# A post-norm block with routed experts: six batches instead of five in the first feed-forward pass

## The chip, the cores and the metric

The kernel runs on one core of one Trainium2 chip. The metric is device time in microseconds (us) of one execution. An execution that is profiled carries its own time, which need not be that of the runs without a profile.

## What is computed

The input is 8 batches of 256 tokens with 128 channels, float32. The reference, cut to its skeleton:

```python
x = layernorm(x + attn_A(x))            # 16 heads of 8, one key/value head, rotary, causal
h = x + attn_B(rmsnorm(x, g1))          # 16 heads of 64, 4 key/value heads, rotary, causal
y = h + moe(rmsnorm(h, g2))
out = layernorm(x + y)

def moe(x):                             # n = 2048 tokens
    logits = x @ router_w + router_b
    vals, idx = top_k(logits, 2);  scores = softmax(vals)
    oh  = one_hot(idx, 8)
    pos = cumsum(cumsum(oh, axis=0), axis=1)      # place of the token in its expert's queue
    emask = oh * (pos < 256)                      # an expert takes 255 at most
    m = max over the two choices of (emask * expert number)
    y = ff_m(x)                                   # one expert a token: gelu(x@w2 * x@w1) @ w3
    slot = where(token was taken, y, x)
    return sum of slot * scores
```

The place of a token in an expert's queue depends on all tokens before it, and on none after it. So the first batches can be routed before the last ones are known.

## The kernel before, in words

**Steps.** `step(s)` for s = -4 to 7 runs software-pipelined stages: both attentions of several batches interleave. In step s the second attention's scores and values are those of batch s (stage SB), and its output projection, residual, norm and router logits are those of batch s-1 (stage TB). Steps 6 and 7 are thin: the first attention has ended, and step 7 has only SB and TB. Step 7 also projects batch 7 itself (`project_out(7)` finishes batch 6, `project_out(NB)` batch 7). Every engine has its own instruction list in a fixed order, and waits on semaphores.

**The feed-forward** works on tiles of 128 slots, each slot a token, each tile one expert. It has two passes, `PASSES`: before, tiles 0 to 9 of the 16 token tiles (batches 0 to 4) and tiles 10 to 15 (batches 5 to 7). A pass of n token tiles needs n + 7 slot tiles at most, so `COUNT` is 17 and 13: 30 tiles, taken two at a time in 16 groups (`GROUPS`), 9 in the first pass, whose last has one tile, and 7 in the second.

**Routing of a pass** on VectorE (DVE): `first_choices` (L1463 to L1474, 13 instructions), then `counts` on TensorE (PE; L831, L834), `admit` (DVE, L1483 to L1492), `ranks` (PE, L845, L848), `slots` (DVE, L1516 to L1540; after L1528 the indices `sidx` are there), `shares` (DVE, L1499 to L1506). GpSimd (POOL) then writes the tokens to their slots in memory, one indirect DMA a token tile (`scatter`, L563, each waiting for the landing of the one before the last), loads the slots back four tiles at a time (`load_slots`, L571), and multiplies the tokens by the share that they keep (`keep_inputs`, L577). `turn_slots` (PE, L1071) and `take_slots` (ScalarE, ACT) transpose a group's slots, `find_experts` (L1081) loads its experts' numbers into registers, `up` (L1095) begins it. Then follow ACT's `copy`, DVE's `gate` (L1562), ACT's `gelu`, PE's `turn_hidden` (L1105), DVE's `take_hidden` (L1569), PE's `down` (L1115), DVE's `take_outputs` (L1577), and a DMA to memory (SyncE, SP).

**Where the first pass is routed.** `ROUTED[0]` is step 6: counts and ranks stand between the score and value matmuls of step 6, scatter and loads at the end of POOL's step 6.

**The end.** When all outputs of the first pass are in memory, POOL gathers them, one indirect DMA a token tile (`gather`, L583). DVE adds them in two parts (`add_outputs(0)` and `(1)`, L1598 and L1602) behind its work of groups 14 and 15, before it takes the last group's hidden values. The rows of the second pass are gathered after the last group; then come `add_outputs(2)`, `(3)`, the last layernorm (L1608 to L1615) and the output's DMA.

The lines that set this:

```python
NB0 = NB - 3
GATHERS = [(0, 5), (5, 10), (10, 13), (13, 16)]
FINAL = [(0, 10), (10, 13), (13, 16)]
ROUTED = [NB - 2, NB]
```

Of the kernel before, what the change touches and what calls it, by code (L numbers as in the profile page):

```python
# [32 lines left out]
NB, T, C = 8, 256, 128  # L33
# [8 lines left out]
CAP = NB * T // E  # L42
EPS_LN, EPS_RMS = 1e-5, 1e-6
NEG = -1e30
NB0 = NB - 3
PASSES = [(0, NB0 * NT), (NB0 * NT, NTILES)]
PARTS = PASSES
COUNT = [hi - lo + E - 1 for lo, hi in PASSES]
# [3 lines left out]
GROUPS = [(i, list(range(START[i] + k, START[i] + min(k + 2, COUNT[i])))) for i in range(2) for k in range(0, COUNT[i], 2)]  # L52
NG = len(GROUPS)
NG0 = (COUNT[0] + 1) // 2
CHUNKS_X = [[(START[i] + k, START[i] + min(k + 4, COUNT[i])) for k in range(0, COUNT[i], 4)] for i in range(2)]
GATHERS = [(0, 5), (5, 10), (10, 13), (13, 16)]
FINAL = [(0, 10), (10, 13), (13, 16)]
QA = DA * (H + 1)
QB = (H + HKV) * DB

# [19 lines left out]
AHEAD = {"PA": 4, "MA": 3, "SA": 3, "TA": 2, "PB": 2, "MB": 1, "SB": 0, "TB": -1}  # L80
FIRST = -AHEAD["PA"]
ROUTED = [NB - 2, NB]
IN_STEP = {NB - 2: {"bv0": [(NB - 2, "bv0"), (NB - 2, "cnt0")], "sm0": [(NB - 2, "sm0"), (NB - 2, "rk0")]},
           NB - 1: {"sm0": [(NB - 1, "ws00"), (NB - 1, "ws01")], "bv3": [], "bo0": [], "bo1": [], "xfT": [], "lg": [],
                    "sm1": [(NB, "xg0"), (NB - 1, "ws10"), (NB - 1, "ws11"), (NB - 1, "bv3"),
                            (NB - 1, "bo0"), (NB - 1, "bo1"), (NB, "bo0"), (NB, "bo1")]}}
BETWEEN = {(0, 0): [(NB - 1, "xfT")], (0, 1): [(NB - 1, "lg")], (1, 0): [(NB, "xfT")], (1, 1): [(NB, "lg")],
           (2, 1): [(NB, "cnt1")], (3, 1): [(NB, "rk1")]}

# [98 lines left out]
def build(nc, x, Wq, bq, Wk, bk, Wv, bv, Wo, bo, g1, g2, wq, wk, wv, wo, router_w, router_b,  # L188
          w1, w2, w3, cf, cb, out):
    with ExitStack() as ctx:  # L190
# [454 lines left out]
        def _(pe):  # L645
# [323 lines left out]
            def step(s):  # L969

                on = stages(s)
                if s == FIRST:
                    pe.wait_ge(x0_in, 16)
                if s == FIRST + 1:
                    pe.wait_ge(x_in, 16)
                    pe.wait_ge(c_in, C_IN)
                    pe.wait_ge(wo_in, 16)
                    pe.wait_ge(bias_in, BIAS_OPS)
                if s + AHEAD["MB"] == 0:
                    pe.wait_ge(prep, 3)  # L980
                if s + AHEAD["PB"] == 0:
                    pe.wait_ge(wb_in, WB_IN)
                if "SB" in on:
                    pe.wait_ge(n_dma, 32 * (s + 1))
                scores(s, 0)
                if "TA" in on:
                    turn_values(s)
                maxima_a(s, 0, 2)
                maxima(s, 0, 2)
                if "TA" in on:  # L990
                    turn_out(s)
                if "SB" in on:
                    pe.wait_ge(v_in, s + 1)
                values(s, 0)
                if s == ROUTED[0]:
                    counts(0)
                maxima_a(s, 2, 4)
                if "TA" in on:
                    project_out_a(s)
                maxima(s, 2, 4)  # L1000
                values(s, 1)
                weights(s, 0)
                if s == ROUTED[0]:
                    ranks(0)
                scores(s, 1)
                maxima_a(s, 4, 6)
                maxima(s, 4, 6)
                values(s, 2)
                maxima_a(s, 6, 8)
                max_rows_a(s, 0)  # L1010
                scores(s, 2)
                if "PB" in on:
                    pe.wait_ge(xn_in, s + AHEAD["PB"] + 1)
                    turn_x(s, "bx", xn)
                if "TB" in on and s < NB - 1:
                    project_out(s)
                maxima_a(s, 8, 10)
                maxima(s, 6, 8)
                if "PB" in on:
                    project(s, 0)  # L1020
                if "SA" in on:
                    scores_a(s, 0)
                maxima_a(s, 10, 12)
                if s == NB - 1:
                    turn_slots(0, *GROUPS[0])
                    find_experts(0)
                    weights(s, 1)
                    values(s, 3)
                    project_out(s)
                    project_out(NB)  # L1030
                else:
                    values(s, 3)
                    max_rows_a(s, 1)
                    weights(s, 1)
                maxima(s, 8, 12)
                if "PB" in on:
                    project(s, 1)
                if "SA" in on:
                    scores_a(s, 1)
                if "MB" in on:  # L1040
                    max_rows(s)
                if "PA" in on:
                    n = s + AHEAD["PA"]
                    turn_x(s, "ax", x_all[:, NT * n:NT * (n + 1), :])
                if "SA" in on:
                    values_a(s, 0)
                if "PA" in on:
                    project_a(s)
                if "TB" in on and s < NB - 1:
                    turn_tokens(s)  # L1050
                if "PB" in on:
                    turn_qk(s, 0)
                if "SA" in on:
                    scores_a(s, 2)
                if "TB" in on and s < NB - 1:
                    logits(s)
                if "PB" in on:
                    turn_qk(s, 1)
                if "SA" in on:
                    values_a(s, 1)  # L1060
                if "PA" in on:
                    turn_qk_a(s)
# [89 lines left out]
        def _(dve):  # L1152
# [466 lines left out]
            def between(n, half):  # L1619

                if (n, half) == (0, 1):
                    take_logits(NB - 1, NB - 2)
                if (n, half) == (1, 1):
                    take_logits(NB, NB - 1)
                    first_choices(1)
                if (n, half) == (2, 1):
                    admit(1)
                if (n, half) == (3, 1):
                    slots(1)
                if (n, half) == (8, 1):  # L1630
                    shares(*PASSES[1], 2)
                if (n, half) == (10, 1):
                    dve.wait_ge(z_in, NB)
                    add_kept(0, 5, 1)
                if (n, half) == (11, 1):
                    add_kept(5, 10, 1)
                if (n, half) == (12, 1):
                    add_kept(10, 16, 3)
                if (n, half) == (14, 1):
                    add_outputs(0)  # L1640
                if (n, half) == (15, 1):
                    add_outputs(1)
# [29 lines left out]
        def _(act):  # L1672
# [112 lines left out]
            def step(s):  # L1785
# [26 lines left out]
                exp(s, 5)  # L1812
                if "TB" in on and s < NB - 1:
                    inverse_root(root_t, var_t, ln_t, r0_t, m + 1)
                if s == NB - 1:
                    take_slots(0, GROUPS[0][1])
                if "SA" in on:
                    exp_a(s, 0)
                    exp_a(s, 1)
# [58 lines left out]
                nc.scalar.activation(hid[:, n % 2, 0:t, :], gated[:, n % 2, 0:t, :], ACT.Gelu).then_inc(hid_in, 1)  # L1878

            nc.scalar.preload_act_table_set("gelu_and_others")  # L1880
            for n, (i, g) in enumerate(GROUPS):
                copy(n, g)
                if n < 2:
# [30 lines left out]
```

## Time and profile before

| | |
|---|---|
| median of 3 runs | 573.47 us (573.19 to 574.51) |
| the profiled execution's own time | 579.19 us |
| its span | 577.3 us |
| PE busy | 481.7 us, 83% |
| DVE, ACT, POOL busy | 387.3 us (67%), 227.8 us (39%), 161.6 us (28%) |
| step 7's first score matmul, from the span's start | 454.61 us |
| first `up` of the feed-forward | 485.43 us |
| last `down` ends | 555.9 us |

The span is the time from the first to the last record; the execution's own time has 1.9 us around it. All times of day below count from the span's start.

### The profile page before, as it was taken

What the parts mean: (1) busy time and instruction counts of PE and PEld (TensorE: products, weight loads), DVE (VectorE), ACT (ScalarE), POOL (GpSimd) and SP (SyncE); (2) the same over time, 40 slices, a digit from 0 to 9 for tenths busy, and PEclk for the clock granted to TensorE, in tenths of its full rate; (3) what the DMA queues carried; (4) which work ended last, traced back from release to release, by engine and by line L of the source; (5) the groups of instructions that cost most, each with busy time, mean ns of one, the idle gap of its engine ahead of it and who ended that gap; (6) DMA issues with size and microseconds to landing.
All of it is one profiled execution on the core that took longest, in us unless ns stands there. A gap on an engine that the chain in (4) does not pass through costs nothing.

```text
span 577.3 us, 8112 instructions
## 1 busy us (share of the span) xinstructions
PE 481.7 (83%) x2788; PEld 266.8 (46%) x2788; DVE 387.3 (67%) x1096; ACT 227.8 (39%) x420; POOL 161.6 (28%) x200
## 2 busy tenths in 40 slices
PE   3766887799999999999999999999879688978820
PEld 2324353454354545535553645455445336645520
DVE  3517779757768676686767686676876266755585
ACT  1242351554473354427424733642333232435300
POOL 4210411400413241124304232222335360062521
PEclk9978997999999999999999999999889799999965
DMA  7400000000020003000300200030341520031213
GB/s 212 157 2 1 1 2 1 3 1 1 3 64 14 0 4 76 1 3 3 73 2 3 63 13 2 3 74 1 119 104 33 154 86 1 19 112 36 74 43 89
DMA packets 19093, 23.82 MB, mean 41 GB/s; under 512 B 2630, under 2 KB 15374, under 8 KB 18158
## 3 DMA queue, kind: packets, MB, share of 16 engines
q1 hardware_dynamic: 15308, 18.19, 12.0%
q0 software_dynamic: 1648, 4.07, 2.5%
q10 hardware_dynamic: 2098, 1.05, 0.6%
q8 instruction: 23, 0.38, 0.3%
q14 instruction: 16, 0.13, 0.1%
HBM read 16.71 MB, written 6.28 MB: 40 GB/s over the span
## 4 chain that ended last, share of the span: by engine, by line
PE 64%; DVE 14%; ACT 9%; issue 5%; DMA 4%; POOL 2%; ACTq 1%; another core or an unknown queue 0%; POOLq 0%; DVEq 0%; SPq 0%
PE ps_r L929 8%; PE ps_st L894 6%; PE ps_r L956 6%; PE ps_r L661 5%; PE ps_r L803 4%; ACT pt L1689 4%; PE ps_st L883 4%; PE ps_r L784 3%; PE ps_r L945 3%; PE ps_r L714 3%; DMA pt<-ys_dram,gidx 3%; PE ps_st L696 2%; PE ps_r L965 2%; PE ps_r L908 2%; PE ps_st L1095 2%
## 5 line engine op out<-in xcount | busy, mean ns | idle before, releaser
L554 POOL TENSOR_TENSOR qkr<-qkr,prod 128x512 f32<-128x512 f32 (+1 forms) x48 | 52.3, 1094 | 203.7 <-DVE prod L1309 202.7
L1193 DVE TENSOR_REDUCE rmax_a<-ps_r 128x2 f32<-128x512 f32 (+1 forms) x96 | 61.8, 685 | 20.2 <-PE ps_r L784 19.7
L1689 ACT ACTIVATE pt<-ps_st 128x1024 f32<-128x1024 f32 x48 | 46.5, 1022 | 70.8 <-PE ps_st L699 70.8
L1193 DVE TENSOR_REDUCE rmax<-ps_r 128x2 f32<-128x512 f32 (+1 forms) x96 | 61.1, 683 | 11.5 <-PE ps_r L908 10.6
L661 PE MATMUL ps_r<-cbt 128*128 128x256 bf16 (+1 forms) x192 | 63.6, 331 | 4.5 <-DVE rmax_a L1193 2.3
L1698 ACT ACTIVATE pt<-ps_st 128x1024 f32<-128x1024 f32 x48 | 47.2, 1022 | 37.6 <-PE ps_st L894 36.3
L591 POOL TENSOR_TENSOR oT<-pvb,oT 128x1024 f32<-128x1024 f32 x14 | 33.3, 2398 | 87.3 <-DMA oT<-inv_dram 87.3
L929 PE MATMUL ps_r<-pt,vb 128*64 128x512 f32 x192 | 48.3, 609 | 4.7 <-ACT pt L1698 2.9
L956 PE MATMUL ps_r<-wqkv,xT_b 128*128 128x512 f32 x96 | 45.5, 611 | 3.8 <-DVE rmax_a L1193 3.2
L784 PE MATMUL ps_r<-kq_a 128*128 128x512 f32 x96 | 47.2, 551 | 0.0
L661 PEld LDWEIGHTS ps_r<-cbt 128*128 128x128 bf16 x192 | 19.0, 99 | 48.8 <-issue 33.0
L894 PE MATMUL ps_st<-qbuf,kbuf 64*128 64x512 f32 x288 | 40.8, 416 | 0.0
L714 PE MATMUL ps_r<-pt,va 128*32 128x512 f32 x192 | 26.3, 653 | 9.2 <-ACT pt L1689 6.3
L1755 ACT ACTIVATE pvb<-ps_r 128x512 f32<-128x512 f32 x32 | 19.0, 594 | 36.5 <-PE ps_r L929 36.4
L894 PEld LDWEIGHTS ps_st<-qbuf,kbuf 64*128 64x128 f32 x288 | 26.0, 190 | 15.1 <-issue 10.8
L1306 DVE TENSOR_TENSOR qkr<-ps_r,cft 128x512 f32<-128x512 f32 (+1 forms) x48 | 28.4, 593 | 2.7 <-PE ps_r L956 2.7
L1321 DVE TENSOR_TENSOR qbuf<-ps_r,qbuf 128x512 fp32r<-128x512 f32 x32 | 20.8, 685 | 11.6 <-ACT qbuf L1773 11.5
L956 PEld LDWEIGHTS ps_r<-wqkv,xT_b 128*128 128x128 f32 x96 | 18.1, 198 | 21.8 <-issue 15.1
L883 PE MATMUL ps_st<-nrow,cbt 128*128 128x512 bf16 x96 | 26.3, 399 | 1.8 <-DMA nrow<-negmax 1.8
L908 PE MATMUL ps_r<-kbuf,qbuf 128*128 128x512 f32 x64 | 26.6, 488 | 0.0
L803 PE MATMUL ps_r<-wob,oT 128*128 128x128 f32 x224 | 26.4, 276 | 0.0
L803 PEld LDWEIGHTS ps_r<-wob,oT 128*128 128x128 f32 x224 | 25.6, 192 | 1.2 <-issue 1.2
(237 smaller groups left out, 901.3 us busy)
## 6 DMA issues: line engine op xcount, KB each, us to landing
oT<-inv_dram SPq DMA_DIRECT2D x14, 512.0 KB, 5.8
xs_dram<-pvb SPq DMA_DIRECT2D x1, 2048.0 KB
pt<-in_L_ffn_w SPq DMA_DIRECT2D x2, 1024.0 KB, 7.7
ys_dram<-qkr SPq DMA_DIRECT2D x14, 128.0 KB
qkr<-xs_dram POOLq DMA_DIRECT2D x4, 256.0 KB, 4.0
x_all<-in_L_attn_x ACTq DMA_DIRECT2D x1, 896.0 KB, 8.1
pvb<-xs_dram POOLq DMA_DIRECT2D x3, 256.0 KB, 3.8
out<-x_all SPq DMA_DIRECT2D x1, 640.0 KB
```

The lines of the kernel that those rows point to most:

```text
L554: nc.gpsimd.tensor_tensor(part, part, prod[:, (3 * t + i) % 2, 0:w], ALU.add).then_inc(add_in, 1)
L661: nc.tensor.matmul(o[:, :, P * (i >= 4):], ident_b, qmask.unsqueeze(1).broadcast_to([P, heads, P]), start=True, stop=False, skip_group_che ...
L714: mm = nc.tensor.matmul(o[RG * a:RG * (a + 1), :], va[n % 2][:, kt, :], pt_a(kind)[:, 4 * a:4 * a + 4, :], start=i == 0, stop=i == len(blo ...
L784: nc.tensor.matmul(o, q, k, start=False, stop=True, skip_group_check=True).then_inc(full, 1)
L803: mm = nc.tensor.matmul(o[:, 0:C], of, wob[:, j, :], start=j == 0, stop=j == H // 2 - 1)
L883: nc.tensor.matmul(o[b], top_row if kind == OFF else add_row, nrow[:, G * hk:G * (hk + 1), P * qt:P * (qt + 1)], start=True, stop=False)
L894: mm = nc.tensor.matmul(o[b], k, q, start=False, stop=ql, tile_position=(DB * b, 0))
L929: mm = nc.tensor.matmul(o[DB * b:DB * (b + 1), :], vb[s % 2][:, kt, hk, :], pt_b(kind)[:, G * hk:G * (hk + 1), :], start=j == 0, stop=j == ...
L956: nc.tensor.matmul(o, xT_b[:, P * t:P * (t + 1)], wqkv[:, 512 * i:512 * (i + 1)], start=True, stop=True).then_inc(full, 1)
L1193: nc.vector.tensor_reduce(heads_of(i), ps_r[:, b, :].rearrange("p (h k) -> p h k", h=4 if i < 4 else 2), AX.X, ALU.max).then_inc(free[b], 1)
L1689: nc.scalar.activation(pt_a(kind)[:, 8 * half:8 * half + 8, :], ps_st[:, c % 2, :, :].rearrange("p b (h t) -> p (b h) t", h=4), ACT.Exp, s ...
L1698: nc.scalar.activation(pt_b(kind)[:, 8 * half:8 * half + 8, :], ps_st[:, c % 2, :, :].rearrange("p b (h t) -> p (b h) t", h=4), ACT.Exp, s ...
```

## The change

Six batches are in the first pass and two in the second: 12 and 4 token tiles, 19 and 11 slot tiles, again 30 tiles in 16 groups, of which 10 are now in the first pass. The first pass is routed in step 7. The transposition of group 0's slots and the register loads stand behind the last output projection on PE, and their copy stands behind ACT's table load.

```diff
-NB0 = NB - 3
+NB0 = NB - 2
...
-GATHERS = [(0, 5), (5, 10), (10, 13), (13, 16)]
-FINAL = [(0, 10), (10, 13), (13, 16)]
+GATHERS = [(0, 6), (6, 12), (12, 14), (14, 16)]
+FINAL = [(0, 12), (12, 14), (14, 16)]
...
-ROUTED = [NB - 2, NB]
-IN_STEP = {NB - 2: {"bv0": [(NB - 2, "bv0"), (NB - 2, "cnt0")], "sm0": [(NB - 2, "sm0"), (NB - 2, "rk0")]},
...
+ROUTED = [NB - 1, NB]
+IN_STEP = {NB - 1: {"bv0": [(NB - 1, "bv0"), (NB - 1, "cnt0")],
+                    "sm0": [(NB - 1, "ws00"), (NB - 1, "ws01"), (NB - 1, "rk0")], "bv3": [], "bo0": [], "bo1": [], "xfT": [], "lg": [],
...
                 if s == NB - 1:
-                    turn_slots(0, *GROUPS[0])
-                    find_experts(0)
                     weights(s, 1)
                     values(s, 3)
                     project_out(s)
                     project_out(NB)
+                    turn_slots(0, *GROUPS[0])
+                    find_experts(0)
...
-                    add_kept(0, 5, 1)
+                    add_kept(0, 6, 1)
                 if (n, half) == (11, 1):
-                    add_kept(5, 10, 1)
+                    add_kept(6, 12, 1)
                 if (n, half) == (12, 1):
-                    add_kept(10, 16, 3)
+                    add_kept(12, 16, 3)
...
-                if s == NB - 1:
-                    take_slots(0, GROUPS[0][1])
...
             nc.scalar.preload_act_table_set("gelu_and_others")
+            take_slots(0, GROUPS[0][1])
```

On POOL, over steps 6 and 7 (L591 is the attention output times its divisors, of batch 5 and then of batch 6; L621 keeps the normed tokens of a batch):

```order
 L591 TENSOR_TENSOR oT<-pvb,oT 128x1024 x2
-L563 DMA xs_dram<-x_all,sidx 6144x128 x10
-L571 DMA qkr<-xs_dram 128x4x128 x4
-L571 DMA qkr<-xs_dram 128x128
 L621 COPY x_all<-xf 128x256
 L591 TENSOR_TENSOR oT<-pvb,oT 128x1024 x2
-L577 TENSOR_TENSOR x_all<-x_all,kz 128x128 x10
+L563 DMA xs_dram<-x_all,sidx 6144x128 x12
+L571 DMA qkr<-xs_dram 128x4x128 x4
+L571 DMA qkr<-xs_dram 128x3x128
+L577 TENSOR_TENSOR x_all<-x_all,kz 128x128 x12
 L621 COPY x_all<-xf 128x256
```

The scatters and loads moved one step later, directly ahead of the multiplications, and batch 6's copy L621 now stands behind all of them.

On DVE, in step 7 of the changed kernel, from the end of `admit` to the indices (L1422 to L1425 are the second attention's divisors of batch 7's first half, L1432 its division):

```order
L1492 TENSOR_TENSOR chosen<-cft,slot 128x96
L1422 STREAM_TRANSPOSE vb<-ps_r 128x512
L1424 RECIPROCAL inv_t<-vb 128x16
L1425 STREAM_TRANSPOSE smb<-inv_t 128x512
...
L1432 TENSOR_TENSOR wqkv<-pvb,smb 128x512 x2
L1516 TENSOR_TENSOR kz<-ps_r,cft 128x32
...
L1526 TENSOR_REDUCE slot<-kz 128x12
L1527 SCALAR_TENSOR_TENSOR slot<-slot,cft 128x12
L1528 SCALAR_TENSOR_TENSOR sidx<-slot 128x12
```

Before, step 7 had only the rows L1422 to L1432 of these; the others stood in step 6, with 10 tiles instead of 12.

On PE, the start of the feed-forward in the changed kernel (L803 is the output projection, L1095 is `up(0)`):

```order
L929 MATMUL ps_r<-pt,vb 64x512 x4
L803 MATMUL ps_r<-wob,oT 128x128 x16
L803 MATMUL ps_r<-wob,wqkv 128x128 x9
...
L803 MATMUL ps_r<-wob,pvs 128x128
L1071 MATMUL ps_r<-cft,qkr 128x128 x2
L1081 TENSOR_LOAD tmap
L1081 ISA x8
L1095 ISA
```

Before, the rows of L1071 and L1081 stood three blocks earlier, ahead of the second half's divisor matmuls (L862).

## Rows read from the trace of the kernel before

**Rows 1.** Chain of waits in order of time: start, duration, what

```profile
451.87 2.69 DMA nrow<-negmax
...
564.82 3.42 DMA pt<-ys_dram,gidx
```

**Rows 2.** Timeline of PE, step 6: start, duration, instruction, idle before and its releaser

```profile
424.82 0.32 PE L831 MATMUL ps_r<-oh_b,cbt 128*128 128x160 bf16 x1 [3.28 <-DVE ru L1474]
...
438.39 3.84 PE L803 MATMUL ps_r<-wob,oT 128*128 128x128 f32 x32
```

**Rows 3.** Timeline of DVE, the routing in step 6, and step 7's first instruction

```profile
425.77 0.33 DVE L1483 COPY kz<-ps_r 128x160 f32<-128x160 f32 x1 [1.01 <-PE ps_r L834]
...
428.06 0.24 DVE L1492 TENSOR_TENSOR chosen<-cft,slot 128x80 bf16<-128x80 f32 x1
...
430.17 0.19 DVE L1516 TENSOR_TENSOR kz<-ps_r,cft 128x32 f32<-128x32 f32 x1 [0.67 <-PE ps_r L848]
...
431.25 2.00 DVE L1521 TENSOR_SCALAR kz<-kz 128x8 f32<-128x8 f32 x1
...
434.32 0.17 DVE L1528 SCALAR_TENSOR_TENSOR sidx<-slot 128x10 uint32<-128x10 f32 x1
```

**Rows 4.** DMA queues by line: issuer, count, size, median us from issue to landing

```profile
qkr<-xs_dram POOLq DMA_DIRECT2D x4, 256.0 KB, 4.0
...
nrow<-negmax SPq DMA_DIRECT2D x4, 4.0 KB, 1.7
```

**Rows 5.** Timeline of PE, step 7 and feed-forward

```profile
454.61 1.89 PE L883 MATMUL ps_st<-nrow,cbt 128*128 128x512 bf16 x4 [1.82 <-DMA nrow<-negmax]
...
459.29 2.06 PE L929 MATMUL ps_r<-pt,vb 128*64 128x512 f32 x8 [0.24 <-ACT pt L1698]
...
492.43 0.60 PE L1105 MATMUL ps_r<-cft,flat 128*128 128x128 f32 x4
...
514.87 1.98 PE L1095 MATMUL ps_st<-pt,xT_b 128*128 x4 [2.41 <-ACT xT_b L1859]
...
546.34 1.16 PE L1095 MATMUL ps_st<-pt,xT_b 128*128 x2 [2.85 <-ACT xT_b L1859]
```

**Rows 6.** Timeline of DVE, step 7

```profile
462.24 0.72 DVE L1422 STREAM_TRANSPOSE vb<-ps_r 128x512 f32<-128x512 f32 x1 [8.39 <-PE ps_r L862]
...
465.81 4.13 DVE L1432 TENSOR_TENSOR wqkv<-pvb,smb 128x512 f32<-128x512 f32 x2
...
479.00 0.69 DVE L1432 TENSOR_TENSOR wqkv<-pvb,smb 128x512 f32<-128x512 f32 x1 [0.53 <-ACT pvb L1755]
```

**Rows 7.** Timeline of POOL, step 6 to the gathers

```profile
428.51 4.72 POOL L591 TENSOR_TENSOR oT<-pvb,oT 128x1024 f32<-128x1024 f32 x2 [13.93 <-DMA oT<-inv_dram]
435.35 1.19 POOL L563 DMA_INDIRECT xs_dram<-x_all,sidx  x1 [2.12 <-issue]
...
451.22 3.62 POOL L571 DMA_DIRECT2D qkr<-xs_dram  x5 [1.87 <-DMA xs_dram<-x_all,sidx]
...
469.35 4.07 POOL L577 TENSOR_TENSOR x_all<-x_all,kz 128x128 f32<-128x128 f32 x10
...
532.24 1.06 POOL L583 DMA_INDIRECT pt<-ys_dram,gidx  x1 [4.90 <-DMA ys_dram<-qkr]
...
545.47 0.94 POOL L583 DMA_INDIRECT pt<-ys_dram,gidx  x1 [0.42 <-issue]
558.50 0.94 POOL L583 DMA_INDIRECT pt<-ys_dram,gidx  x1 [12.08 <-DMA ys_dram<-qkr]
```

**Rows 8.** Busy time by stretch: stretch, length, PE, PEld, DVE, ACT, POOL, PEclk, DMA, GB/s

```profile
450.00:460.00 10.00, 6.73 (x29) 3.75 (x29) 1.52 (x3) 2.53 (x4) 4.02 (x6) 0.66 0.59 164
```

**Rows 9.** Timeline of DVE, the end

```profile
551.56 1.39 DVE L1598 SCALAR_TENSOR_TENSOR x_all<-pt,kz,x_all 128x128 f32<-128x128 f32 x5
552.98 1.06 DVE L1602 BATCH_NORM_STATS2 kz<-x_all 128x6 f32<-128x128 f32 x5
...
573.13 1.63 DVE L1615 TENSOR_SCALAR x_all<-x_all,kz 128x128 f32<-128x128 f32 x6
```

More of the change, by code:

```diff
@@ L81 @@
 FIRST = -AHEAD["PA"]
-ROUTED = [NB - 2, NB]
-IN_STEP = {NB - 2: {"bv0": [(NB - 2, "bv0"), (NB - 2, "cnt0")], "sm0": [(NB - 2, "sm0"), (NB - 2, "rk0")]},
-           NB - 1: {"sm0": [(NB - 1, "ws00"), (NB - 1, "ws01")], "bv3": [], "bo0": [], "bo1": [], "xfT": [], "lg": [],
-                    "sm1": [(NB, "xg0"), (NB - 1, "ws10"), (NB - 1, "ws11"), (NB - 1, "bv3"),
-                            (NB - 1, "bo0"), (NB - 1, "bo1"), (NB, "bo0"), (NB, "bo1")]}}
+ROUTED = [NB - 1, NB]
+IN_STEP = {NB - 1: {"bv0": [(NB - 1, "bv0"), (NB - 1, "cnt0")],
+                    "sm0": [(NB - 1, "ws00"), (NB - 1, "ws01"), (NB - 1, "rk0")], "bv3": [], "bo0": [], "bo1": [], "xfT": [], "lg": [],
+                    "sm1": [(NB - 1, "ws10"), (NB - 1, "ws11"), (NB - 1, "bv3"),
+                            (NB - 1, "bo0"), (NB - 1, "bo1"), (NB, "bo0"), (NB, "bo1"), (NB, "xg0")]}}
 BETWEEN = {(0, 0): [(NB - 1, "xfT")], (0, 1): [(NB - 1, "lg")], (1, 0): [(NB, "xfT")], (1, 1): [(NB, "lg")],
```

## The prediction

> **What bounds the kernel now.** I read the chain of waits first, then the timelines of PE, DVE and POOL from step 6 to the end. The change touches three places. In step 6 the routing lies on the path: PE stands still for 3.28 us before the counts, because DVE is computing them [rows 2]. In step 7 the path goes over PE and ACT's exponentials and never meets a routing: the slots have long been loaded, and `up(0)` starts at 485.43. At the end the path goes over the gathers: after the last group POOL issues six, one each 1.26 us (from 558.50, [rows 7], to 564.82, [rows 1]), and the last lands 3.42 us after its issue [rows 1]. So the change trades a shorter step 6 and a shorter tail for a routing in the thinnest step of the program, whose cover must be checked.
>
> **Step 6: gain.** PE's first value matmuls end at 421.54 (3.28 before 424.82), and scores begin again at 429.92. What stays between them is two mask-and-maximum groups, half a value group and half a divisor group, 1.0 us each (eight value matmuls take 2.06, [rows 5]; the others have as many columns). That makes 424.5, a gain of 5.4. The output projection, at 438.39 [rows 2], would come to 433.0, but it needs POOL's product, which ends at 428.51 + 4.72 = 433.2 [rows 7]; the gain shrinks to 5.1. Behind it nothing waits for a routing. Step 7 begins when the row of maxima has landed, 2.69 us here [rows 1] while scatters and loads were in flight; the median of such transfers is 1.7 [rows 4], and these others are gone: 0.5 more. Step 7 starts at 454.61 - 5.6 = 449.0.
>
> **Step 7: loss.** I count from its first score matmul [rows 5], in us:
> - The first half of the value matmuls ends at 5.7 (459.29 - 454.61 and half of 2.06, [rows 5]). `first_choices` has finished before that: 13 short DVE instructions against 5.7 us of cover.
> - 12 counts matmuls: the first of the old ones takes 0.32 [rows 2]; they overlap, so all cost between nothing and 12 x 0.32. Their columns (1248) need 0.5 at 2.4 GHz, so 0.6, near the lower end. 6.3.
> - `admit`: 425.77 to 428.30 for 10 tiles [rows 3], 2.5; with 12 tiles, and its start, 2.9. 9.2.
> - Divisors of batch 7's first half: 462.24 to 465.81 [rows 6], 3.6. 12.8. They are now queued behind `admit`, and PE is not hurt, since the second half's divisors come at 20.
> - The division: two instructions. Before they took 4.13, beside POOL's product; one alone takes 0.69 [rows 6]. POOL's product starts earlier, since its transfer no longer shares the queues with the loads, so I take 1.4, and keep 4.1 as the bound. 14.2.
> - `slots` to the indices: 430.17 to 434.49 [rows 3] is 4.3, in which one 128x8 instruction took 2.00 while POOL worked. Its neighbours take 0.2, and POOL is idle here: 2.6. 16.8. The first scatter's record begins 0.86 after the indices (434.49, 435.35): 17.6.
> - Scatters: ten from 435.35 to 451.22 - 1.87 = 449.35 [rows 7], 14.0; twelve 16.5. 34.1. Landing of the last 1.87. 36.0.
> - The first four slot tiles land 4.0 after issue [rows 4]. 40.0. PE has had nothing to do since the output projections' end (485.43 + 1.3 for their move, so 32.1). Transposes, ACT's copy and the register loads, which now stand on the path (below 0.97 us: they hid in an idle time of that size): 41.5.
> - A second branch: POOL issues five loads (3.62), multiplies 12 tiles (4.07 for 10, so 4.9, [rows 7]) and only then copies batch 6's tokens (as much as one multiplication, 0.4). 45.0. DVE cannot write batch 7's normed tokens before that copy, and `gate(0)` is queued behind this on DVE. Writing 0.6, gate 0.7, gelu 0.6: PE can turn group 0's hidden values at 47.0.
> - PE's clock. In the stretch around step 7's start the granted clock is 0.66 of full, and the first four matmuls took 1.89 [rows 5, 8], about twice what their columns need at full speed: the lower of its two levels, 1.2 and 2.4 GHz. PE stood idle there before for some microseconds; now it stands idle for about eight before `up(0)`. I add 1.0 to the second branch, between 0 (the branch over POOL hides it) and 2.3 (both `up` at half clock). 48.0.
>
> Before, this point was at 492.43 - 454.61 = 37.8 [rows 5]. Step 7 loses 10.2; with the 5.6 of step 6 the feed-forward is **4.6 late**.
>
> **The feed-forward.** 30 tiles in 16 groups as before: nothing, but the second pass's routing works on four token tiles, some 30 DVE instructions with 16 columns fewer. 80 columns take 0.24 and 32 take 0.19 [rows 3], so each is some 0.015 shorter: **-0.4**.
>
> **The gathers of the first pass: loss.** They start when the first pass's last outputs are in memory. That was group 8, now it is group 9: one group later, 3.6 us, so at 535.9 in before's time (532.24, [rows 7]). The pitch is (545.47 - 532.24) / 9 = 1.47 [rows 7], the last landed 2.3 after its issue. Twelve end at 535.9 + 11 x 1.47 + 2.3 = 554.4. DVE wants them at 551.56 [rows 9], with one tile more in the first part 552.1: it waits 2.3, adds six tiles instead of five (1.39 + 1.06 for five, so 0.5 more), and passes its last hidden values on 0.5 + 2.3 + 0.5 = 3.2 later. PE's `down(15)`, the outputs and the last gathers are all behind this.
>
> In that execution PE twice stood 2.41 and 2.85 us before an `up`, ACT having waited for nothing that the profile shows [rows 5]. The profiled execution took 579.19, the median 573.47, which is 5.7 more; the two stalls are 5.3. I take them for a cost of that execution. Without the second, DVE is at `add_outputs(1)` 2.8 earlier, but the gathers are not: the loss is 3.2 + 2.8 = **6.0**. 3.2 stays as the lower bound.
>
> **The tail: gain.** Two gathers fewer after the last group, 2 x 1.26 = 2.5 [rows 1, 7]. Behind the last landing DVE adds two tiles instead of three and normalises four instead of six: 0.28 + 0.22 and 0.5 (1.63 for six, [rows 9]). Aggregates and a smaller output I put at 0.4, between nothing and 1: **-3.9** in all. DVE's layernorm of twelve tiles instead of ten costs 0.7, beside the gathers' landing.
>
> **Sum.** +4.6 - 0.4 + 6.0 - 3.9 = +6.3. Against the profiled execution the same terms give 579.19 + 3.5 (with 3.2 for the gathers) = 582.7; against the median, 573.47 + 6.3 = 579.8.
>
> **A page's price.** The four slot tiles take 4.0 from issue to landing [rows 4]. The Trainium skill, DMA: Bandwidth & Descriptors, on the anatomy of a DMA of the gpsimd path, fits 2.0 us and the bytes over 436 GB/s: 2.6 for 256 KB. By it `up(0)` is 1.4 earlier, but the branch over POOL hides most of that: the sum would be 579.0.
>
> **Rivals.**
> 1. The step 7 loss is larger. The division runs beside POOL's product and takes 4.13 as before [rows 6], or the 2.00 of the 128x8 instruction comes again [rows 3], or step 6 gives back less. For it: POOL's product depends on a transfer whose time varies. Against: its start is at about 7 and its length 4.7, so it is over at 12. It decides if that product still runs at 12.8. +2.8, so 582.6. The Trainium skill, SBUF — State Buffer, on who interferes with whom, says that a DVE instruction with two SBUF inputs and a GpSimd one that reads SBUF block each other wholly; by this rule the 4.13 comes back whenever they overlap. The row of 4.13 agrees, and cannot say whether they will overlap.
> 2. The stalls of the profiled execution are in every run. Then DVE comes late by itself and the gathers cost 3.2: 577.0.
> 3. Faster. Step 7 hides the routing: scatters follow at their own length of 1.0 (3.6 less), the first slots land early and the cold clock costs nothing, so that `up(0)`'s group is no later than before, and the gathers follow at the last six's pitch of 1.26, which leaves a loss of 3.0. 573.47 - 0.4 + 3.0 - 3.9 = 572.2. It decides if group 0's slots are there 4.6 sooner, at 35.4 in step 7. For it: the waits between scatters were one of 1.6 in ten. Against: the pitch of ten scatters was 1.4.
> 4. The change does not shorten step 6 (another wait takes its place, such as POOL's product), and the rest holds in part: 584 and above.
>
> **How the numbers follow.** Forecast 579.8, 0.46 (578 to 582). Rival 1 0.16, rival 2 0.18, rival 3 0.12, rival 4 0.03; 0.05 for a result between 572.3 and 574.6, which is no change: 0.2% (1.15 us) is about what a measurement of this kernel tells from none. Slower is then 0.83, same 0.05, faster 0.12. The range leaves out rival 3 and what lies beyond rival 1: 574.0 to 584.0.
>
> **What the profile would show.** Right: step 7 starts at about 449; PE idle some 8 us before `up(0)`, at about 490; DVE's first instruction of `add_outputs(1)` with an idle time ended by a gather; four gathers at the end. Wrong: no idle time of PE between the last projection and `up(0)`, a step 7 that starts later than 452, or `add_outputs(1)` without a wait for a gather.

## The result and the profile after

The changed kernel took **580.78 us** (median of 12 runs, 576.6 to 585.61), the kernel before on the same chip 574.8 (12 runs, 567.54 to 577.23). The ratio is **1.0125 [1.0084, 1.0167]**: slower. Forecast were 579.8 us and +6.3; the medians differ by +6.0. Measured again later, the ratio was 1.0117 [1.002, 1.0213] (experiment 11). Ratios leave out the runs in the slower of the chip's two states and medians do not, so a ratio need not be the quotient of the medians beside it.

The profiled execution took 577.67, 3.1 less than its kernel's median; that of before took 579.19, 4.4 more than its own. The page, its span, busy time and chain:

```profile
span 575.8 us, 8114 instructions
...
PE 481.1 (84%) x2790; PEld 265.6 (46%) x2790; DVE 381.1 (66%) x1096; ACT 228.2 (40%) x420; POOL 160.5 (28%) x199
...
PE 60%; DVE 14%; DMA 8%; ACT 6%; issue 6%; POOL 4%; ACTq 1%; POOLq 0%; SPq 0%; DVEq 0%
```

PE's work is what it was (481.7 before). The chain of before gave PE 64%, DMA 4% and POOL 2%; now scatters and gathers hold more of it.

PE's timeline in the changed kernel (start, duration, instruction, idle before and its releaser):

```profile
446.88 1.89 PE L883 MATMUL ps_st<-nrow,cbt 128*128 128x512 bf16 x4 [0.87 <-DMA nrow<-negmax]
...
485.63 0.69 PE L1071 MATMUL ps_r<-cft,qkr 128*128 128x128 f32 x2 [6.53 <-DMA qkr<-xs_dram]
487.75 3.78 PE L1095 MATMUL ps_st<-pt,xT_a 128*128 x4 [1.42 <-ACT xT_a L1857]
...
495.08 0.60 PE L1105 MATMUL ps_r<-cft,flat 128*128 128x128 f32 x4
...
549.62 0.69 PE L1105 MATMUL ps_r<-cft,flat 128*128 128x128 f32 x2 [4.45 <-ACT flat L1876]
...
557.76 1.22 PE L1115 MATMUL ps_r<-pvb,pvs 128*128 x4 [5.75 <-DVE pvs L1569]
```

The first row answers to [rows 5]: step 7 starts 7.7 earlier. The second is the new hole of PE, 6.5 us for the first slots. `up(0)` then takes 3.78 for four matmuls, 1.9 elsewhere: the lower clock (granted 0.50 in this stretch), after that idle time. `turn_hidden(0)` is at 495.08, 2.65 later than before. The last two are waits behind the gathers.

DVE's timeline in the changed kernel:

```profile
455.79 0.26 DVE L1492 TENSOR_TENSOR chosen<-cft,slot 128x96 bf16<-128x96 f32 x1
...
459.53 2.21 DVE L1432 TENSOR_TENSOR wqkv<-pvb,smb 128x512 f32<-128x512 f32 x2
...
464.02 0.17 DVE L1528 SCALAR_TENSOR_TENSOR sidx<-slot 128x12 uint32<-128x12 f32 x1
...
545.70 1.66 DVE L1598 SCALAR_TENSOR_TENSOR x_all<-pt,kz,x_all 128x128 f32<-128x128 f32 x6 [1.88 <-DMA pt<-ys_dram,gidx]
...
554.21 1.66 DVE L1598 SCALAR_TENSOR_TENSOR x_all<-pt,kz,x_all 128x128 f32<-128x128 f32 x6 [4.16 <-DMA pt<-ys_dram,gidx]
```

Both parts of `add_outputs` now wait for a gather, 1.88 + 4.16 = 6.0. Before, neither did: the second is in [rows 9], and this is the first, from DVE's timeline of the kernel before:

```profile
547.76 1.39 DVE L1598 SCALAR_TENSOR_TENSOR x_all<-pt,kz,x_all 128x128 f32<-128x128 f32 x5
```

POOL's timeline in the changed kernel:

```profile
455.84 4.75 POOL L591 TENSOR_TENSOR oT<-pvb,oT 128x1024 f32<-128x1024 f32 x2 [15.07 <-DMA oT<-inv_dram]
465.05 1.19 POOL L563 DMA_INDIRECT xs_dram<-x_all,sidx  x1 [4.46 <-issue]
...
482.27 3.81 POOL L571 DMA_DIRECT2D qkr<-xs_dram  x5 [1.86 <-DMA xs_dram<-x_all,sidx]
...
490.35 0.39 POOL L621 COPY x_all<-xf 128x256 f32<-128x256 f32 x1
...
535.76 1.07 POOL L583 DMA_INDIRECT pt<-ys_dram,gidx  x1 [9.22 <-DMA ys_dram<-qkr]
...
551.56 0.94 POOL L583 DMA_INDIRECT pt<-ys_dram,gidx  x1 [0.37 <-DMA pt<-ys_dram,gidx]
```

Counted from step 7's start, the scatters run from 18.2 to 33.5 and the loads are issued at 35.4 (forecast 17.6, 34.1, 36.0). The gathers' pitch is (551.56 - 535.76) / 11 = 1.44 (forecast 1.47). In this execution POOL's product of batch 6 starts at 455.84, 0.05 after DVE has begun the last instruction of `admit` (455.79). In others it starts before that.

### The profile page after: what moved, and what is told of

Its sections match the earlier page's. It is cut to its first block, busy times and chain, and to the rows that moved or that the text cites. A ratio compares the mean times of both kernels' runs of the same rounds, so it can differ in the third digit from the quotient of the medians.

```text
span 575.8 us, 8114 instructions
## 1 busy us (share of the span) xinstructions
PE 481.1 (84%) x2790; PEld 265.6 (46%) x2790; DVE 381.1 (66%) x1096; ACT 228.2 (40%) x420; POOL 160.5 (28%) x199
## 4 chain that ended last, share of the span: by engine, by line
PE 60%; DVE 14%; DMA 8%; ACT 6%; issue 6%; POOL 4%; ACTq 1%; POOLq 0%; SPq 0%; DVEq 0%
PE ps_r L929 6%; PE ps_r L956 6%; PE ps_st L894 5%; PE ps_r L661 5%; ACT pt L1689 4%; PE ps_r L803 4%; DMA pt<-ys_dram,gidx 3%; PE ps_r L784 3%; PE ps_st L883 3%; PE ps_r L945 3%; PE ps_r L714 3%; PE ps_st L1095 3%; PE ps_st L696 2%; PE ps_st L699 2%; DVE rmax_a L1193 2%
## 5 line engine op out<-in xcount | busy, mean ns | idle before, releaser
L591 POOL TENSOR_TENSOR oT<-pvb,oT 128x1024 f32<-128x1024 f32 x14 | 32.9, 2370 | 93.6 <-DMA oT<-inv_dram 93.6
L929 PE MATMUL ps_r<-pt,vb 128*64 128x512 f32 x192 | 48.2, 607 | 4.4 <-ACT pt L1698 2.7
L956 PEld LDWEIGHTS ps_r<-wqkv,xT_b 128*128 128x128 f32 x96 | 18.1, 198 | 21.7 <-issue 15.1
L1443 DVE TENSOR_TENSOR y<-ps_r,x_all 128x128 f32<-128x128 f32 x16 | 4.6, 291 | 33.9 <-PE ps_r L803 33.9
L803 PE MATMUL ps_r<-wob,oT 128*128 128x128 f32 x224 | 26.3, 276 | 0.7 <-POOL oT L591 0.7
L803 PEld LDWEIGHTS ps_r<-wob,oT 128*128 128x128 f32 x224 | 25.6, 192 | 1.9 <-issue 1.9
```

The source lines that it names most:

```text
L591: ins = nc.gpsimd.tensor_tensor(oT[:, k], pvb[1 - u][:, k, :, :].rearrange("p t (g c) -> p t g c", g=G), oT[:, k], ALU.mult)
L803: mm = nc.tensor.matmul(o[:, 0:C], of, wob[:, j, :], start=j == 0, stop=j == H // 2 - 1)
L929: mm = nc.tensor.matmul(o[DB * b:DB * (b + 1), :], vb[s % 2][:, kt, hk, :], pt_b(kind)[:, G * hk:G * (hk + 1), :], start=j == 0, stop=j == ...
L956: nc.tensor.matmul(o, xT_b[:, P * t:P * (t + 1)], wqkv[:, 512 * i:512 * (i + 1)], start=True, stop=True).then_inc(full, 1)
```

## Experiments

Ratios are against the kernel before, run on the same chip. The theory is that of the prediction: three prices, the first slots' late arrival, the cold clock, and the waits for the gathers, against a shorter step 6 and tail. The rival is a larger step 7 loss.

**1. Five batches, routed in step 7.** The place alone (with the slots turned behind the last projection), without the sixth batch.

```diff
-NB0 = NB - 2
+NB0 = NB - 3
-GATHERS = [(0, 6), (6, 12), (12, 14), (14, 16)]
+GATHERS = [(0, 5), (5, 10), (10, 13), (13, 16)]
...
```

> Only the place of the routing is changed: five batches in the first pass as before, but routed in step 7, group 0's slots turned behind the last projection. Theory (the loss is the sum of a late routing, which step 6 pays back, and of a longer wait for the gathers of the first pass): step 7 starts about 7 us earlier than before, the feed-forward's first group is as late as before (two scatters and two tiles of routing less than in the changed kernel, 2.9 us), gathers and tail are those of before. Ratio 1.000, within 0.997 to 1.004. Rival (the whole loss is the routing in step 7): ratio 1.008 or more.

Measured: 578.92, ratio 1.0041 [1.001, 1.0072], at the upper end of what the theory allowed. So the place costs 0.4%, and the sixth batch about 0.8% more (1.0125 against 1.0041; the intervals do not meet). With it come two more scatters, and two more gathers that start a group later. The profile has a row that no forecast had, at `admit`'s last instruction, which begins 0.03 after POOL's product (455.00). DVE's timeline:

```profile
455.03 2.41 DVE L1492 TENSOR_TENSOR chosen<-cft,slot 128x80 bf16<-128x80 f32 x1
```

This instruction takes 0.24 where POOL is idle [rows 3]. Below, "the collision" means this meeting of POOL's product with `admit`.

**2. The second part of `add_outputs` behind the last group's outputs.**

```diff
-                if (n, half) == (15, 1):
-                    add_outputs(1)
...
             take_outputs(NG - 1, GROUPS[NG - 1][1])
+            add_outputs(1)
```

> The changed kernel, with DVE's second addition of the first pass's outputs (tiles 6 to 11) moved behind the copies of the last group's outputs, so that DVE does not wait for the gathers ahead of the last group's hidden values. Theory (this wait is on the path): the last outputs are copied some 6.5 us earlier, and 1.6 to 3 us come back because the addition now stands before the last layernorm: about 3.4 us faster than the changed kernel, ratio to the kernel before 1.0065 (1.004 to 1.009). Rival (the tail is bound by the gathers' transfers anyway): ratio 1.0125 as the changed kernel.

Measured: 581.44, ratio 1.0085 [1.0049, 1.0121] (one of the seven executions took 2565.83 and is not in the ratio): 0.4% less than the changed kernel's 1.0125, some 2.3 us of the 4.16 that DVE waited. The intervals overlap, so the medians alone do not show this gain. The profiles agree with it: from `turn_hidden(0)` to the end of the span 78.3 us, against 80.7 in the first profile of the changed kernel and 81.1 in that of experiment 11. In the tail DVE waits 1.17 for a gather before the moved part.

The profile shows something else that the edit has no part in. Beside the first pass's scatters DVE stands 6.1 us in the middle of the output projection, although PE's matmuls for it ended at 473.69. Batch 7's norm comes late by that, and on ACT the table load and the copy of the first slots stand behind it. So `up(0)` waits 3.62 for that copy (1.42 in the first profile). DVE's and PE's timelines:

```profile
479.70 0.29 DVE L1443 TENSOR_TENSOR y<-ps_r,x_all 128x128 f32<-128x128 f32 x1 [6.11 <-remote]
```

```profile
488.17 3.78 PE L1095 MATMUL ps_st<-pt,xT_a 128*128 x4 [3.62 <-ACT xT_a L1856]
```

What held DVE is open.

**3. `slots` ahead of the division.** It is meant to bring the indices 5.7 us sooner.

```diff
                     admit(0)
+                    slots(0)
...
-                    slots(0)
                     shares(*PASSES[0], 1)
```

> The changed kernel, with slots(0) on DVE ahead of the divisors and the division of batch 7's first half. Theory (the chain counts, admit, divisors, division, slots, twelve scatters, load sets the start of the feed-forward): the indices are there 5.7 us earlier, the scatters start when POOL's product has ended, about 4.0 us earlier, and so does up(0): ratio to the kernel before 1.0055 (1.003 to 1.008). Rival (PE's order of work in step 7, not the slots, sets it): no change, 1.0125, since the divisors come later.

Measured: 583.29, ratio 1.012 [1.0088, 1.0153]: no gain, the rival's number. PE's timeline, at the ranks and the scores behind them:

```profile
462.30 0.22 PE L845 MATMUL ps_r<-chosen,cbt 128*128 128x96 bf16 x1 [1.94 <-DVE chosen L1492]
...
462.71 1.87 PE L883 MATMUL ps_st<-nrow,cbt 128*128 128x512 bf16 x4
```

DVE's `chosen` took 2.13 beside POOL's product, PE stood for it with the ranks at the head of its queue, and its next matmuls ran at half clock. The indices came 15.1 after step 7's start, against 17.3 in the first profile and 20.8 in that of experiment 11, which had the collision too. What they gave was lost behind batch 7's norm, which now ended last: DVE stood 3.50 in the output projection as in experiment 2, and `up(0)` waited 4.46 for ACT's copy.

**4. Group 0's slots turned ahead of the output projections, as before.** ACT's copy moves with them.

```diff
+                    turn_slots(0, *GROUPS[0])
+                    find_experts(0)
                     weights(s, 1)
                     values(s, 3)
                     project_out(s)
                     project_out(NB)
-                    turn_slots(0, *GROUPS[0])
-                    find_experts(0)
...
```

> The changed kernel with the turning of group 0's slots and the register loads back ahead of the second half's divisor matmuls in step 7, and ACT's copy with them. Theory: PE stands about 20 us at the slots' arrival (from 465 to 485), and then has 13 us of divisors, values and projections to do before up(0): some 10 to 12 us slower than the changed kernel, near 591. Rival (the move is a matter of tidiness): as the changed kernel.

Measured, in two executions: 594.78, ratio 1.0323 [1.0262, 1.0384]. PE's timeline:

```profile
490.01 0.69 PE L1071 MATMUL ps_r<-cft,qkr 128*128 128x128 f32 x2 [18.07 <-DMA qkr<-xs_dram]
492.02 5.59 PE L862 MATMUL ps_r<-pt,cft 128*64 128x512 f32 x16 [1.32 <-issue]
```

PE stands 18 us with batch 7's weights and values and both projections queued behind, and that work begins at a lower clock (5.59 for the 16 matmuls that take 3.65 elsewhere). Moving the turns was what made the late routing bearable: worth 2%.

**5. Five batches, routed in step 6 as before, but counts and ranks later in the step.** The gain that step 6 offers, without the loss of step 7.

```diff
-IN_STEP = {NB - 2: {"bv0": [(NB - 2, "bv0"), (NB - 2, "cnt0")], "sm0": [(NB - 2, "sm0"), (NB - 2, "rk0")]},
+IN_STEP = {NB - 2: {"sm0": [(NB - 2, "sm0"), (NB - 2, "cnt0")], "bv2": [(NB - 2, "bv2"), (NB - 2, "rk0")]},
...
```

(`counts`, `ranks`, `admit`, `slots` and `shares` move with it.)

> The kernel before, still five batches routed in step 6, but counts on PE stand behind the first half's divisors and ranks behind the third value matmuls; on DVE admit stands behind the second maxima and slots and shares behind the third. Theory (PE's 3.28 us of waiting and its cold clock behind it were the cost of the routing in step 6, and the routing itself has cover there): step 7 starts about 6 us earlier, everything behind it too: ratio 0.990 (0.987 to 0.994). Rival (step 6 is bound by DVE's maxima and POOL's product, so that the wait turns up elsewhere): ratio 1.000.

Measured: 575.76, the kernel before 580.36, ratio 1.0016 [0.995, 1.0083]: inconclusive. So it was run again. (The expectation below speaks of slots turned behind the last projection; the kernel is that of experiment 5, which leaves them where they were.)

> Five batches in the first pass with the slots turned behind the last output projection, once more, since the interval of its first measurement reached over 1: ratio 0.988 to 0.994, if placing the turns there is worth what the shorter step 6 gives; rival 0.998 to 1.002.

Measured: 574.07, the kernel before 578.49, ratio 0.9942 [0.9907, 0.9977]. Faster than the kernel before in this measurement; the two intervals share 0.995 to 0.9977, so the gain is about 0.4% and less than the 1% that was expected. In PE's timeline of this run step 7 starts 1.5 before [rows 5], where 6 was expected:

```profile
453.11 1.89 PE L883 MATMUL ps_st<-nrow,cbt 128*128 128x512 bf16 x4 [1.00 <-DMA nrow<-negmax]
```

**6. The kernel before with `add_outputs(1)` late**, the edit of experiment 2.

> The kernel before, with the second addition (tiles 5 to 9) moved behind the copies of the last group's outputs. Theory: in that kernel the addition hardly waits for a gather, so only its own 2.45 us leave the path, and the tail has room for them: ratio 0.996. The gain is smaller than the same edit's in the changed kernel (3.4). Rival: no change in either.

Measured: 579.81, ratio 0.9956 [0.9912, 1.0001], an interval that just reaches 1: the same 0.4% as with six batches. That edit is no cure for the sixth batch in particular.

**7. Experiments 5 and 6 together.**

> Both edits in the kernel before: routing later in step 6, second addition behind the last outputs. Theory: the gains add, 6 + 2.5 us: ratio 0.985 (0.981 to 0.990). Rival: the feed-forward's earlier start is lost again at the gathers; ratio 0.990.

Measured: 573.97, ratio **0.9881 [0.9826, 0.9935]**: the lowest of all. It keeps the routing in the step whose queues are full.

**8. Six batches with all repairs**: experiments 2 and 3, and batch 6's tokens copied on POOL ahead of the multiplications.

```diff
-                if s == NB - 1:
-                    pool.wait_ge(share_in, 1)
-                    keep_inputs(*PASSES[0], xf_all)
                 if "TB" in on:
                     pool.wait_ge(xf_in, m + 1)
                     nc.gpsimd.tensor_copy(xf_all[:, NT * m:NT * (m + 1), :], xf[:, :, :]).then_inc(xfa_in, 1)
+                if s == NB - 1:
+                    pool.wait_ge(share_in, 1)
+                    keep_inputs(*PASSES[0], xf_all)
```

> Six batches in the first pass with slots(0) first, the second addition behind the last outputs, and batch 6's copy ahead of the multiplications on POOL. Theory: 4.0 + 3.4 us faster than the changed kernel: ratio to the kernel before 0.9995 (0.996 to 1.003), so slower than five batches with a later routing (0.985). Rival: one of the two gains only, 1.006.

Measured: 581.02, ratio 0.9991 [0.9955, 1.0026]: no slower than before, and behind experiment 7. In the profiled execution, an unusually long one (585.9), DVE's addition for batch 7's residual, with both inputs in SBUF, was held while POOL's twelve multiplications (4.52) ran:

```profile
488.66 4.58 DVE L1446 TENSOR_TENSOR x_all<-x_all,y 128x256 f32<-128x256 f32 x1
```

It takes 0.43 in the kernel before, and 0.57 beside the same multiplications in experiment 3, so why it was held for the whole time here is open. `up(0)` waits 7.79 for the copy behind it.

**9. Does the clock cost?** The changed kernel with 28 matmuls whose products nobody reads, in PE's wait for the first slots.

```diff
                     project_out(NB)
+                    pe.wait_ge(probs_b, NB * E_B)
+                    for _ in range(28):
+                        nc.tensor.matmul(ps_st[:, 1, 1, :], ident_b, cbt[:, 0:512], start=True, stop=True)
                     turn_slots(0, *GROUPS[0])
```

> The changed kernel with 28 extra matmuls of 512 columns, whose products nobody reads, between the last output projection and the first turn of the slots, in the wait of TensorE for the first tokens. It tests the clock term of the prediction: TensorE stands still from about 479 to 486 us, and up(0) then runs at 3.78 us a piece of four instead of 1.9. If the half clock there is due to the idle stretch, up(0) and gate(0) run at the full clock, turn_hidden(0) comes 3 to 5 us earlier where PSUM and POOL allow it and at least 1 us earlier in any case, and the ratio against the kernel before falls from 1.0125 to 1.005 to 1.010. Rival: turn_hidden(0) is held by the chain of the slots' turns on DVE and POOL, not by TensorE's clock, or the clock does not follow the extra work: ratio 1.011 to 1.014.

Measured: 585.31, ratio 1.0133 [1.0058, 1.0207]; the changed kernel on the same chip (experiment 11) 1.0117. PE's timeline (lines behind the filler are numbered 3 higher):

```profile
490.02 6.21 PE L1031 MATMUL ps_st<-cbt 128*128 128x512 bf16 x28
496.06 0.38 PE L1074 MATMUL ps_r<-cft,qkr 128*128 128x128 f32 x2
...
498.11 1.98 PE L1098 MATMUL ps_st<-pt,xT_a 128*128 x4 [1.67 <-ACT xT_a L1860]
```

The clock followed: 1.98 for `up(0)` instead of 3.78. But the extra work ended at 496.1, about 3 us after the slots had landed (the loads were issued at 489.67, and in experiment 11 PE had its slots 3.56 after that issue). `turn_hidden(0)` came 14.0 after the loads' issue, against 13.3 in experiment 11 and 12.8 in the first profile. So the turn came 3 us later and the hidden values only 0.7 to 1.2; from the turn of the slots to the hidden values 7.6 us, against 9.5 in the first profile. By this the half clock costs about 2 us there, and a filler of this length gives them away again. The gain that I expected did not appear, and the ratio is the rival's; a shorter filler was not tried.

**10. Four semaphores for the gathers**, so that each waits for the gather four back.

```diff
-                if k > 1:
-                    pool.wait_ge(yg_even_odd[k % 2], 16 * (k // 2))
-                gather(k, 0, yg_even_odd[k % 2])
+                if k > 3:
+                    pool.wait_ge(yg_even_odd[k % 4], 16 * (k // 4))
+                gather(k, 0, yg_even_odd[k % 4])
...
```

> The changed kernel with the semaphores of the first pass's gathers divided into four instead of two, so that the queue waits for the gather four back and not two back. If the gathers' pitch of 1.44 us comes from their landings (the landing of k-2 before k), it falls to about 1.26 us, the twelfth lands some 2 us earlier, and the waits of 1.88 and 4.16 us for the gathers shrink to some 4 in sum: ratio 1.007 to 1.011. Rival: the pitch is the queue's own work, and nothing changes: ratio 1.0125.

Measured: 585.61, ratio 1.0151 [1.009, 1.0211]: no gain. POOL did what was expected:

```profile
542.65 1.07 POOL L583 DMA_INDIRECT pt<-ys_dram,gidx  x1 [9.01 <-DMA ys_dram<-qkr]
...
556.53 0.94 POOL L583 DMA_INDIRECT pt<-ys_dram,gidx  x1 [0.30 <-issue]
```

Pitch (556.53 - 542.65) / 11 = 1.26. But the other engines stood still meanwhile. The timeline of all engines, the same kernel:

```profile
553.09 1.71 PE L1095 MATMUL ps_st<-pt,xT_b 128*128 x2 [2.96 <-issue]
...
559.72 0.42 DVE L1577 COPY qkr<-ps_r 128x256 f32<-128x256 f32 x1 [6.41 <-remote]
559.76 0.38 ACT L1868 ACTIVATE prod<-ps_st 128x256 f32<-128x256 f32 x1 [6.31 <-remote]
```

ACT could have read `ps_st` at 554.8, where PE's last `up` ends, and DVE its row at 557.2; both went on at 559.7, 2.2 after POOL's last gather instruction. The wait for gathers, 6.0 in all, had become zero, but from `turn_hidden(0)` to the last output copy it took 66.95, against 64.22 in experiment 11. What held ACT and DVE stays open. This profile also has the collision, and in step 7 `up(0)` waits 5.09 for ACT's copy, as in experiment 2.

**11. The changed kernel again.**

> The changed kernel once more, on the chip of the other runs of this call, so that they can be compared with it: ratio 1.009 to 1.016.

Measured: 586.88, ratio 1.0117 [1.002, 1.0213]; its six runs lie at 580.7, 581.6, 585.8, 588.0, 590.0 and 590.8. This profile, of 585.75, shows the collision most fully. DVE's timeline in step 7:

```profile
456.40 0.55 DVE L1487 SCALAR_TENSOR_TENSOR kz<-kz 128x96 f32<-128x96 f32 x2
456.98 2.58 DVE L1489 TENSOR_TENSOR kz<-kz,cft 128x96 f32<-128x96 f32 x2
459.60 2.28 DVE L1490 TENSOR_TENSOR kz<-kz 128x96 f32<-128x96 f32 x1
...
465.94 1.29 DVE L1432 TENSOR_TENSOR wqkv<-pvb,smb 128x512 f32<-128x512 f32 x2
```

POOL's:

```profile
457.06 4.70 POOL L591 TENSOR_TENSOR oT<-pvb,oT 128x1024 f32<-128x1024 f32 x2 [14.28 <-DMA oT<-inv_dram]
```

And PE's:

```profile
448.89 1.46 PE L883 MATMUL ps_st<-nrow,cbt 128*128 128x512 bf16 x3 [1.28 <-DMA nrow<-negmax]
...
462.52 0.26 PE L845 MATMUL ps_r<-chosen,cbt 128*128 128x96 bf16 x1 [4.12 <-DVE chosen L1492]
...
463.18 1.87 PE L883 MATMUL ps_st<-nrow,cbt 128*128 128x512 bf16 x4
464.98 2.93 PE L894 MATMUL ps_st<-qbuf,kbuf 64*128 64x512 f32 x12
...
495.89 3.36 PE L1095 MATMUL ps_st<-pt,xT_a 128*128 x4 [2.09 <-ACT xT_a L1857]
```

POOL's product starts 8.2 us into step 7, before `admit` is over. Two of DVE's two-input instructions then end only when POOL's two have ended (457.06 + 2.35 and + 4.70; DVE's 0.1 later each): 2.58 + 2.28 instead of 0.55 + 0.26, **4.05 us**. PE, with the ranks at the head of its queue, stands 4.12, and its next 16 matmuls run at half clock (1.87 + 2.93 against 1.02 + 1.66 in the first profile).

From step 7's start, against the first profile: the indices at 20.8 (17.3), the loads at 40.7 (35.4), `turn_hidden(0)` at 53.9 (48.2). So 3.5 of the 5.7 were lost before the indices, where the collision's 4.05 is partly paid back by a shorter division (1.29 for 2.21). Another 1.8 was lost between scatters, where POOL once waited 1.88 for a landing.

## Why the prediction was right, and where not

Sign, size and range held. Part by part, the first profile of the changed kernel against that of before:

- **Step 6**, forecast 5.6 earlier, measured 7.7. The mechanism held: from PE's first value matmuls to the second half's scores 4.04 us (419.25 to 423.29), which is what I had (420.46 to 424.5). As forecast, the output projection then waited for POOL's product. The 2.1 that I had not: this product came 0.8 earlier, which was so ahead of the first changed instruction and is no merit of the change. PE's wait for the last maxima fell from 2.46 to 1.59, which I had left as it was. And the row-of-maxima transfer took 1.74 instead of 2.69 (0.95 for my 0.5).
- **Step 7**, forecast a loss of 10.2 up to `turn_hidden(0)` at 48.0; measured 48.2. Within it: `admit` ends at 9.2 as forecast; the division took 2.21 for my 1.4; indices at 17.3 (16.8); scatters at the pitch of (479.44 - 465.05) / 11 = 1.31, for the 1.4 of before that I scaled; loads at 35.4 (36.0); the first transposes at 38.75 (after a landing of 3.36, for the 4.0 of [rows 4]). `up(0)` then at half clock in full, 1.9 more, where I had put 1.0 beside the branch over POOL. That branch was not the longer one: POOL's copy ended at 43.9 (490.35 + 0.39), and DVE wrote batch 7's tokens only at 45.2, behind PE's transposes of batch 6, which stand behind `up(0)`:

```profile
492.09 0.61 DVE L1652 SCALAR_TENSOR_TENSOR xf<-y,root_t_r,g2b 128x128 f32<-128x128 f32 x2 [10.21 <-PE ps_r L812]
```

- **The gathers**: I forecast a loss of 6.0, with 3.2 as the lower bound. DVE's waits are 1.88 + 4.16 = 6.0, but the loss is smaller. The stretch from `turn_hidden(0)` to the last output copy grew by only 0.46 between these two profiles (63.93 against 63.47). In the three profiles of kernels with five batches and no second stall (experiments 1 and 5, and 5 once more) it is 60.0 to 61.3, so the change lengthens it by 2.6 to 3.9, where I had 6.0 - 0.4 = 5.6. What I had wrong are the two stalls of [rows 5], which I took for a cost of one profiled execution. From `up(6)` to `up(7)` pass 5.8 us in the profile of before and 4.3 to 5.8 in all others with five batches, but 3.3 to 3.5 in all those with six. The first stall thus goes with a second pass of six scatters, and the change removes 1 to 2.5 us of it: a gain that I missed. The second, from `up(14)` to `up(15)`, comes and goes: 6.2 in the profile of before, 5.1 and 4.4 in experiments 6 and 7, 3.3 to 3.4 in the three named above. Why PE stands there was not tried.
- **The tail**, forecast -3.9: from the last output copy to the end of the span 575.8 - 559.01 = 16.8, before 577.3 - 555.9 = 21.4: -4.6.
- **Sum for these profiles**: +2.65 (feed-forward), +0.46 (from `turn_hidden(0)` to the last copy), -4.6 (tail) = -1.5, which is the difference of the spans, 575.8 - 577.3. Against the profiled execution I had forecast +3.5 (582.7), so this part of the forecast failed. The medians differ by +6.0, since one profile lies 4.4 above its median and the other 3.1 below. One profile beside one profile would have called this change faster.
- **The step that failed** is in the section on step 7: "`admit`: 425.77 to 428.30 for 10 tiles [rows 3], 2.5; with 12 tiles, and its start, 2.9." For POOL's product my rival 1 put the start "at about 7", which is inside `admit` (6.3 to 9.2), and I asked only whether the *division* would meet it. The Trainium skill, SBUF — State Buffer, on who interferes with whom, has the rule that I quoted for the division; it holds here for `admit`, whose instructions with two SBUF inputs grew from 0.55 and 0.26 to 2.58 and 2.28 while L1487 ahead of the product kept its 0.55.

So rival 1 was right in kind, placed at the wrong instruction, and it comes and goes from one execution to the next: the product starts 8.2 to 9.0 into step 7, and `admit` ends at 8.5 to 9.2 when nothing is in its way. Of the five profiles with step 7 as the change has it (experiments 2, 9, 10, 11 and the first), three show the collision (9, 10, 11). Their indices come at 20.5 to 21.3; in the other two at 16.7 and 17.3.

The collision is not all that differs between them. In four of the five (2, 9, 10, 11) DVE also stands 3.5 to 6.1 us in the output projection beside the scatters, and `up(0)` waits 1.7 to 5.1 for ACT's copy behind batch 7's norm (1.4 in the first). From the loads to `turn_hidden(0)` pass 12.8 us in the first profile, where DVE does not stand, and 17.2, 14.0, 16.5 and 13.3 in the others. So `turn_hidden(0)` stands at 48.2 in the first profile, 52.1 in experiment 2 without any collision, and at 55.1 (with the filler of experiment 9), 56.2 and 53.9 in those with it. The forecast has neither, and the profile on which its parts are tried above is the one of five that has neither.

That the number 6.3 met the median is therefore in part luck. What I missed for the change (2.1 in step 6, and 1.7 to 3.0 behind `turn_hidden(0)`, the first stall included) nearly cancels what I missed against it: the collision and DVE's stand, with which `turn_hidden(0)` comes 3.9 to 8.0 us later in step 7. How often runs without a profile have them is not recorded; that they account for the spread of experiment 11's six runs is argued, not shown. A kernel that keeps POOL's product behind `admit` was not tried.

Of the rivals: 2 (577.0) and 3 (572.2) lie outside the interval of the first measurement, though rival 2 had the first stall right. 4 fell at once, since step 6 was shortened by more than forecast.

## What to carry to other kernels

Where a chain of small instructions is moved beside another engine's long ones, lay both on one clock and ask for every instruction of the chain, not for the largest alone, whether its inputs lie in the memory that those read; a 0.26 us instruction cost up to 2.4 here, and 4.1 on PE, which had the next link at the head of its queue (experiment 11). In this kernel the routing belongs where queues are full: placed later within its own step it gained a little (1.0016 and 0.9942 in two measurements, and 0.9881 with the late addition), moved into the thin last step it lost (1.0041). And compare medians, and more than one profile: two single profiles gave -1.5 where the kernels differ by +6.0, and of five profiles of the same step 7 one alone was without a collision or a stall.

## What the hardware showed unexpectedly

- Two DVE instructions of 0.26 with both inputs in SBUF ended only when the POOL tensor product that ran beside them had ended, one for each of POOL's two: 2.58 for the pair of L1489, then 2.28 (experiment 11); 2.41 in experiment 1, 2.13 in experiment 3. An addition of 0.43 took 4.58 beside twelve POOL multiplications in experiment 8, and 0.57 beside them in experiment 3.
- PE's clock fell to the lower of its two levels after waits of 1.9 (experiment 3), 4.1 (experiment 11) and 6.5 us (the changed kernel): 1.87 against 1.02 for four matmuls, 3.78 against 1.98, with a granted clock of 0.50 in all three, and stayed at the higher one where filler ran through the wait (experiment 9, granted clock 1.00).
- Four gathers in flight instead of two brought their pitch from 1.44 to 1.26, and ACT and DVE stood 6.3 and 6.4 us beside them (experiment 10).
- Beside the twelve scatters DVE stood 6.1 us with its input ready (experiment 2), and 3.5 to 4.1 in experiments 3, 9, 10 and 11; in the first profile it did not. What held it is open.
